# A two-layer graph network: segment sums with h held still, and the destination part of each quad packed on 96 partitions

## The reference

```
m_in  = concat([h_node[src], h_node[dst], h_edge])      # 200000 x 384
m     = silu(m_in @ msg_W1 + msg_b1) @ msg_W2 + msg_b2
agg   = segment_sum(m, dst, 6250)
h_new = silu(concat([h_node, agg]) @ upd_W1 + upd_b1) @ upd_W2 + upd_b2
x1    = layernorm(x + layernorm(h_node + h_new) * gamma + beta)

agg   = segment_sum(x1[src], dst, 6250) / max(deg, 1)
h     = relu(relu(concat([x1, agg]) @ W1 + b1) @ W2 + b2)
out   = layernorm(x1 + h)
```

## Time and profile before

| | us |
|---|---|
| median of 3 runs | 3071.88 |
| lowest, highest | 3070.5, 3090.59 |
| span of the profiled execution | 2569.7 |
| preparation (0 to 82) | 82 |
| edge stage (82 to 2095) | 2013 |
| edge stage's end (2095 to 2107) | 12 |
| node stage and layer 1 (2107 to the end) | 463 |

### The profile page before, as it was taken

The page is one execution under the profiler, slowest core; times in us unless marked ns, Lnnn a source line. Parts: engine busy times, 40 slices in busy tenths (PEclk is TensorE's granted clock), DMA queues, the critical chain, the costliest instruction groups (busy, mean ns, idle before and its releaser), DMA issues. The chain is left out here.

```text
span 2569.7 us, 58924 instructions
## 1 busy us (share of the span) xinstructions
PE 2182.9 (85%) x21030; PEld 1871.4 (73%) x21030; DVE 1577.3 (61%) x4059; ACT 847.9 (33%) x1368; POOL 1664.2 (65%) x1618
## 2 busy tenths in 40 slices
PE   7898888888888988898889888988898878799996
PEld 7786777677777776776777776767677754699994
DVE  4786676667666766676667666766676647600005
ACT  3343333333333433333333333333333326200004
POOL 4777777777777777777777777777777755200002
PEclk9899999899899989998899999999999988899998
DMA  6555545554555555545554555455545543688871
GB/s 236 197 190 190 167 159 185 181 169 154 177 190 173 158 180 181 187 141 180 184 190 139 186 175 190 144 182 176 191 150 176 176 118 96 245 309 302 303 268 51
DMA packets 135225, 471.71 MB, mean 184 GB/s; under 512 B 55730, under 2 KB 77490, under 8 KB 113555
## 3 DMA queue, kind: packets, MB, share of 16 engines
q1 hardware_dynamic: 84586, 368.35, 41.1%
q0 software_dynamic: 50176, 102.86, 14.3%
q10 hardware_dynamic: 426, 0.03, 0.0%
HBM read 369.41 MB, written 101.70 MB: 183 GB/s over the span
## 5 line engine op out<-in xcount | busy, mean ns | idle before, releaser
L519 POOL DMA_INDIRECT gath<-P_d,src_i x1540 | 1543.2, 1002 | 469.4 <-issue 465.5
L650 PE MATMUL ps_pre<-wc,eT 128*128 128x128 f32 x3136 | 702.4, 306 | 13.7 <-DVE counts L567 13.7
L682 PE MATMUL ps_sum<-h,edgeN 128*128 128x129 f32 x3136 | 486.2, 302 | 265.7 <-ACT h L744 265.2
L590 DVE TENSOR_TENSOR pre<-ps_pre,gath 128x512 f32<-128x512 f32 x392 | 265.9, 678 | 588.6 <-issue 548.7
L682 PEld LDWEIGHTS ps_sum<-h,edgeN 128*128 128x128 f32 x3136 | 422.2, 209 | 278.1 <-ACT h L744 277.7
L744 ACT ACTIVATE h<-pre 128x512 f32<-128x512 f32 x392 | 247.9, 632 | 1122.2 <-DVE pre L590 1068.3
L666 PE MATMUL ps_cnt<-edgeK,edgeL 128*128 128x500 bf16 (+1 forms) x3136 | 585.1, 336 | 29.6 <-DVE edgeK L580 29.4
L580 DVE TENSOR_SCALAR edgeK<-iota,key 128x600 bf16<-128x600 f16 (+2 forms) x1568 | 526.4, 396 | 0.0
L652 PE MATMUL ps_pre<-Qw,nodeE 128*128 128x128 bf16 x4704 | 520.4, 220 | 0.0
L650 PEld LDWEIGHTS ps_pre<-wc,eT 128*128 128x128 f32 x3136 | 478.1, 192 | 32.6 <-issue 29.6
L666 PEld LDWEIGHTS ps_cnt<-edgeK,edgeL 128*128 128x128 bf16 x3136 | 320.1, 105 | 199.3 <-DVE edgeK L580 42.8
(11 more groups left out here) (128 smaller groups left out, 1021.4 us busy)
## 6 DMA issues: line engine op xcount, KB each, us to landing
eT<-eT SPq DMA_DIRECT2D x56, 1792.0 KB, 9.2
A_d<-counts SPq DMA_DIRECT2D x56, 1568.0 KB
A_c<-A_d SPq DMA_DIRECT2D x56, 1568.0 KB, 8.1
rel_b<-rel_d SPq DMA_DIRECT2D x56, 896.0 KB
gath<-P_d,src_i POOLq DMA_INDIRECT x1568
Qw<-Q_d SPq DMA_DIRECT2D x56, 96.0 KB
Q_d<-Qst SPq DMA_DIRECT2D x7, 672.0 KB, 7.8
xT_sb<-xT SPq DMA_DIRECT2D x7, 448.0 KB, 8.1
```

Of the source, the lines that this page charges most:

```text
L519: pool.indirect_dma_start(gath[:, q, t * D:(t + 1) * D], None, v["P_d"], bass.IndirectOffsetOnAxis(ap=src_i[k][:, c:c + 1], axis=0)).then_ ...
L590: V.tensor_tensor(pre[x][:], ps_pre[x][:], gath[:, q, :], ALU.add).then_inc(pre_add, 1)
L650: T.matmul(o, eT[k][:, e0:e0 + P], wc[:], start=True, stop=False)
L682: last = T.matmul(ps_sum[k][:, 0:SW], edgeN[x][:, t, :], h[x][:, t, 0:SW], start=(q == 0 and t == 0), stop=(q == GQ - 1 and t == QT - 1))
```

## The change

- **Sums.** `h` is now held still and a one-hot moves: per tile one f32 product of `h` with 40 columns of `edgeN` (f32), so that the sums come out with features on partitions, as `sumT` wants them. `edgeN` covers 40 nodes from `NLO[q]`, not 128. Degrees come from four more products, of a matrix of ones with `edgeB`, the same one-hot in bf16. A product of zeros clears the bank first. ACT's copy of the sums, the transposes and the column of ones are gone. `add_sums` reads the bank itself, at quad 1 of the next group, not at quad 5.
- **One-hot of the block.** `edgeL` is made by four TENSOR_SCALARs of 128 columns.
- **Destination part.** The window is 32 nodes per quad, and its 96 partitions hold (node, part) pairs: partition p holds part p mod 3 of node p // 3. One product of K = 96 takes the place of three. `rel_d` is relative to the quad's first node; `pid` holds p // 3. `nodeE` is made per quad (`expand`, 96 x 512), two quads ahead. `Qw` is loaded by seven DMAs per group, each with its own read of a row number (`qbase`). `rel_b` has two buffers of 96 partitions.
- **Checks.** Each quad has to lie in its 40-node window.

```diff
@@ sizes
+QW = 32
+WN = 40
+NLO = [max(0, 16 * q - 10) for q in range(GQ)]
+KQ = 3 * QW
@@ build_prepare, vector: checks
-            V.tensor_scalar(relR[:], R_i[:, 0:RC], RB_i[:, 0:1], None, ALU.subtract).then_inc(rel_ready, 1)
+            V.tensor_tensor(rows4(relR[:]), rows4(R_i[:, 0:RC]),
+                            RB_i[:].unsqueeze(2).broadcast_to([RP, RQ, QT * P]), ALU.subtract).then_inc(rel_ready, 1)
...
+            for q in range(GQ):
+                V.tensor_scalar(bad[:, 5, q:q + 1], dF[:, q:q + 1], float(NLO[q]), None, ALU.is_lt)
...
+            V.tensor_scalar(qbase[:], orow[:], 3.0, None, ALU.mult)
@@ build_edges, sync
         def load_window(g, k):
 
-            base = sp.value_load(gbase[0:1, bass.ds(g, 1)], min_val=0, max_val=NP_ - 1)
-            sp.dma_start(Qw[k][:], v["Q_d"][bass.ds(base, P), :]).then_inc(q_in[k], 16)
+            for q in range(GQ):
+                base = sp.value_load(qbase[0:1, bass.ds(g * GQ + q, 1)], min_val=0, max_val=3 * NP_ - 3)
+                sp.dma_start(Qw[k][:, q, :], Q3[bass.ds(base, KQ), :]).then_inc(q_in[k], 16)
...
-                    sp.wait_ge(prepared, g + 2)
-                    load_rel(g + 2)
+                    sp.wait_ge(nodes, g * GQ + GQ)
+                    load_rel(g + 2, k)
@@ build_edges, vector
+        def expand(s, q, k, half, first=False):
+
+            x = (k + q) % 2
+            if q == 0:
+                dve.wait_ge(r_in[k], 16 * (half + 1))
+            if not first:
+                dve.wait_ge(pre_mm, s - 1)
+            V.tensor_scalar(nodeE[x][:], rel_b[k][:, q * QT * P:(q + 1) * QT * P], pid[0:KQ, 0:1], None,
+                            ALU.is_equal).then_inc(nodes, 1)
...
-            V.tensor_tensor(edgeN[x][:], io, rel_g[k][:, c].unsqueeze(2).broadcast_to([P, QT, P]), ALU.is_equal)
-            V.tensor_tensor(edgeL[x][:], io, low[k][:, c].unsqueeze(2).broadcast_to([P, QT, P]), ALU.is_equal)
+            io = iota[:, NLO[q]:NLO[q] + WN].unsqueeze(1).broadcast_to([P, QT, WN])
+            rel = rel_g[k][:, c].unsqueeze(2).broadcast_to([P, QT, WN])
+            V.tensor_tensor(edgeN[x][:], io, rel, ALU.is_equal)
+            V.tensor_tensor(edgeB[x][:], io, rel, ALU.is_equal)
+            for j in range(QT):
+                V.tensor_scalar(edgeL[x][:, j, :], iota[:, 0:P], low[k][:, q * QT + j:q * QT + j + 1], None, ALU.is_equal)
...
-            dve.wait_ge(sum_tr, g + 2)
+            dve.wait_ge(sum_mm, (g + 1) * GQ)
@@ build_edges, tensor
                 T.matmul(o, eT[k][:, e0:e0 + P], wc[:], start=True, stop=False)
-                for part in range(3):
-                    last = T.matmul(o, nodeE[k][:, e0:e0 + P], Qw[k][:, part * D:(part + 1) * D],
-                                    start=False, stop=(part == 2))
+                last = T.matmul(o, nodeE[x][:, t * P:(t + 1) * P], Qw[k][:, q, :], start=False, stop=True)
...
             for t in range(QT):
-                last = T.matmul(ps_sum[k][:, 0:SW], edgeN[x][:, t, :], h[x][:, t, 0:SW],
-                                start=(q == 0 and t == 0), stop=(q == GQ - 1 and t == QT - 1))
+                T.matmul(ps_sum[k][:, cols], h[x][:, t, :], edgeN[x][:, t, :], start=False, stop=True, skip_group_check=True)
+            for t in range(QT):
+                last = T.matmul(ps_sum[k][:, P + NLO[q]:P + NLO[q] + WN], onesb[:], edgeB[x][:, t, :], start=False, stop=True,
+                                skip_group_check=True)
```

More of the change, by code:

```diff
@@ L279, in scalar @@
         firsts, lasts = v["dst_first"], v["dst_last"]
[L280 to L283, removed]
+        with nc.allow_non_contiguous_dma(reason="one word for each quad"):
+            act.dma_start(RB_i[:], firsts[0:TILES].rearrange("(r q t) -> r q t", q=RQ, t=QT)[:, :, 0]).then_inc(r_in, 16)
         act.dma_start(F_i[:], bass.AP(firsts.tensor, firsts.offset, [[GT, GROUPS], [1, GT + 1]])).then_inc(t_in, 16)
@@ L418, in build_edges @@
     first_i = [v["first_i0"], sb("first_i1", [P, GT], I32)]
-    nodeE = [sb(f"nodeE{k}", [P, GE], BF16) for k in range(2)]
-    Qw = [sb(f"Qw{k}", [P, 3 * D], BF16) for k in range(2)]
+    rel_b = [v["rel_b0"], sb("rel_b1", [KQ, GE], BF16)]
+    nodeE = [sb(f"nodeE{k}", [KQ, QT * P], BF16) for k in range(2)]
+    Qw = [sb(f"Qw{k}", [KQ, GQ, D], BF16) for k in range(2)]
     rel_g = [sb(f"rel_g{k}", [P, GT]) for k in range(2)]
@@ L425, in build_edges @@
     low = [sb(f"low{k}", [P, GT]) for k in range(2)]
-    edgeN = [sb(f"edgeN{k}", [P, QT, P]) for k in range(2)]
+    edgeN = [sb(f"edgeN{k}", [P, QT, WN]) for k in range(2)]
+    edgeB = [sb(f"edgeB{k}", [P, QT, WN], BF16) for k in range(2)]
     edgeL = [sb(f"edgeL{k}", [P, QT, P], BF16) for k in range(2)]
@@ L606, in group @@
                 add(s, q, k, g, first and q < 2)
+                if q < GQ - 2:
+                    expand(s + 2, q + 2, k, half)
+                elif not last:
+                    expand(s + 2, q + 2 - GQ, nxt[1], nxt[0])
                 if q < GQ - 1:
@@ L611, in group @@
                     hots(s + 1, 0, 1 - k)
-                if not last and q in (2, 3, 4):
-                    if q == 2:
-                        make_keys(*nxt)
-                    else:
-                        (expand_first, expand_rest)[q - 3](*nxt, early=first)
-                if q == 5 and not first:
+                if not last and q == 2:
+                    make_keys(*nxt)
+                if not last and q == 3:
+                    clear(*nxt, early=first)
+                if q == 1 and not first:
                     add_sums(g - 1, 1 - k)
         def fast():
-            for k in range(2):
-                V.memset(h[k][:, :, D:D + 2], 1.0).then_inc(h_ones, 1)
             dve.sem_inc(sum_add, 1)
             make_keys(0, 0, first=True)
-            expand_first(0, 0, early=True)
-            expand_rest(0, 0, early=True)
+            clear(0, 0, early=True)
+            expand(0, 0, 0, 0, True)
+            expand(1, 1, 0, 0, True)
             dve.wait_ge(prepared, 1)
@@ L704, in group @@
                     count(s + 1, 0, k1, g + 1)
-                if q == 1 and not first:
-                    transpose_sums(g - 1, 1 - k)
         def fast():
-            pe.sem_inc(sum_tr, 1)
-            pe.wait_ge(h_ones, 2)
             products(0, 0, 0, 0, True)
```

117 lines of the change are left out of this document (55 added, 62 removed).

## The result

The changed kernel took 3180.09 us (median of 4, 3172.81 to 3189.22) and the kernel before, beside it, 3072.57 (4 runs, 3070.50 to 3090.59): ratio 1.0328, 95% interval 1.0290 to 1.0365. Forecast were 3026 us and a range of 2996 to 3066. The prediction was wrong, in sign too.

What follows compares the result with a forecast made beforehand. The prediction took POOL's back-to-back gathers to bound the edge stage: 49 us less of their waits for VectorE and 3.5 us more at the start make -46 us, so 3026 us from 3071.9, range 2996 to 3066.

Steps and rivals of the forecast that it cites:

- The median of the runs, 3071.9, is 502 us more, which I keep: Whole run: the 502 us between the traced span of 2569.7 us and the median were kept unchanged in the forecast.
- The stage is POOL's row of gathers, back to back: Edge stage: 1540 gathers of 1.002 us, each with 0.305 us before it, make its 2013 us; other engines wait.
- A gather that begins while such an instruction runs waits for that instruction's end, and then goes ahead of the next one: Edge stage, gathers beside VectorE: each waits for one instruction's rest, less about 0.12 us; in all 88 us before.
- The forecast's term: Edge stage: gathers' waits for VectorE instructions fall from 88 to 39 us, 49 us less.
- upper end: Edge stage: gathers' waits after the change are 70 us if nothing falls into step any more, 17 us less.
- If a gather's start fell anywhere at random: Edge stage: an instruction of length L costs (L - 0.126)^2 / (2 x 1.247) us; sums scaled by 0.55.
- The rule of the Trainium skill: Gathers beside VectorE: TENSOR_TENSORs do not stall them, two-port TENSOR_SCALARs do; the sum would be -2 us, not -46.
- The start: Group 0: six more window loads on SP make POOL's first gather of group 1 3.5 us later, once.
- PE's and ACT's savings worth nothing: Edge stage: removed products, transposes and ACT's copy of the sums give 0 us, since the gathers cover them.
- rival 1: Edge stage: new VectorE instructions run without gaps, gathers meet edgeK more, waits fall only 17 us; 3058 us, chance 0.20.
- Rival 3: Edge stage: more idle time lowers PE's clock to 0.65 and PE becomes the bound, +118 us; 3190 us, chance 0.07.

Runs made afterwards that it cites:

- quiet sets: No change to a kernel: sets of runs in which the kernel before took about 2569 us, named after what their traces show.
- halting set: No change to a kernel: a set of runs in which the kernel before took 3072 to 3129 us, named after what its traces show.
- eight products back: Changed kernel with eight more bf16 products per quad on TensorE, onto the same sums with a right side of zeros; 1.0447 of the kernel before.

## Experiments in quiet sets: what the prediction was about

**Instructions added to VectorE's row** (one set, before 2568.92).

```diff
 expand_per_quad             # kernel before; nodeE [P, 512] twice, PE waits for it per quad
+                expand(s + 2, q + 2, k, half)      # behind each add, 128x512
-                        (expand_first, expand_rest)[q - 3](*nxt, early=first)
 vector_034_more             # kernel before
                 add(s, q, k, g, first and q < 2)
+                V.tensor_scalar(spare[3 * k + q % 3][:], iota[:, 0:QT * P], pid[:, 0:1], None, ALU.is_equal)
 expand_bulk                 # changed kernel; nodeE [KQ, GE], two instructions per group
+                        (expand_first, expand_rest)[q - 3](*nxt, early=first)
 no_gathers                  # kernel before; groups 1 to 55 use group 0's rows
-                    pool.indirect_dma_start(
```

> The kernel before with nodeE built per quad, 512 columns right behind each add, where TensorE waits for it, in place of two instructions of 1792 columns per group; three products and one window load stay. The destination part alone cost 144 us, while its eight fewer products gave 39 and seven window loads cost 20, so some 160 us are unexplained. Theory V (a VectorE instruction put into every quad between the add and the one-hots lengthens the chain add, one-hots, counts, add): 0.34 us x 392 = 133 us more, ratio about 1.04 to 1.05. Theory S (only SyncE's loads, the clear and the store cost): within 1% of before. Theory F (each engine starves for instructions now and then, and the number of instructions sets the loss): 5 more VectorE instructions per group, within 1%.

> The kernel before with one VectorE TENSOR_SCALAR of 512 columns more behind each add, into a tile that nobody reads and nobody waits for. Theory V: 0.34 us x 392, ratio 1.03 to 1.045, since the one-hots and so TensorE's counts come later by that. Theory F: one instruction more on VectorE per quad, ratio 1.00 to 1.015. If VectorE has slack, as its 56% of busy time says: 1.00.

> The changed kernel with nodeE built as before in two instructions of 1792 columns per group (on 96 partitions), and the clear of the counts back at the fifth quad. Theory V: 100 us or more come back, ratio to before 0.99 to 1.00. Theory S: the later clear takes the 93 us of waiting for the A_d store away: 1.00 to 1.015. Theory F: no change against the changed kernel, 1.033.

> The kernel before without the gathers of groups 1 to 55 (the adds use group 0's rows, so the result is wrong). In the unchanged kernel run again TensorE's stutters (single matmuls 0.7 us apart with 'issue' gaps, 463 us in the edge stage, in some 130 clusters) end with the last gather. Theory G (POOL's gathers starve the other engines of instructions): no stutter is left, and the edge stage falls from 2485 to 392 x 4.1 = 1610 us, a time near 2200 us. Theory F without the gathers' part: the stutters stay, one cluster in about 110 TensorE records, and the time stays near 3070 us, since the rows are there 35 us before the add anyway.

Measured: 1.0244 (1.0226 to 1.0262), 1.0186 (1.0168 to 1.0205), 1.0241 (1.0223 to 1.0259), 0.832 (0.8303 to 0.8337). This set had no halts, so theories G and F were not put to the test. Theory V's figures, 1.03 to 1.05 for the first two, did not come either: 63 and 46 us, not 133. What the set shows is the quiet kernel: without gathers the time is 431 us less, so the gathers do set the end there.

**The change itself, in a quiet set** (before 2568.23).

> The changed kernel unchanged. If the kernel before takes about 2570 us beside it: theory H (gathers wait through whole rows of back-to-back VectorE instructions, so mean gather 1.04 instead of 1.002) gives 2570 + 60 = 2630 us, as expand_bulk did; the forecast's own theory (a gather waits only for the instruction in which it begins) gives 2524 us; theory K (clock) 2690. If the kernel before takes over 3000 us: 1.033 of it again.

> The destination part alone, unchanged. Without stutters, theory H: expand_per_quad's 1.024 plus what SyncE's window loads add, 1.02 to 1.04. With stutters: 1.048 again.

> The kernel before with the sums part (h stationary, 40 columns) and the block one-hot by four TENSOR_SCALARs, without the destination part. Without stutters, theory H: the four short TENSOR_SCALARs and edgeK stand back to back for 1.9 us per quad, but nodeE is built as before: 1.00 to 1.015; the forecast's theory 0.98. With stutters: the parts gave 1.019 and 1.009 alone, so 1.028 if they add up, less if stutters cost by time and not by part.

> The kernel before without the gathers of groups 1 to 55, unchanged. Without stutters: 0.832 again. With stutters in the kernel before: if they need the gathers, no stutter is left and the time is 2137 us as before, ratio 0.69; if they do not, some 130 stretches stay and the time is 2400 to 3000 us.

Measured: the changed kernel 2840.46 us, 1.1054 (1.1027 to 1.1081); destination part alone 2978.4, 1.1607 (1.1557 to 1.1657); sums and block 0.9974 (0.9957 to 0.9991); no_gathers 0.8313 (0.8295 to 0.833). The change costs 272 us here and 108 in the halting set: it is dearer where my model of the kernel holds. None of the expected figures for it (2630, 2524, 2690 us) came near, nor theory H's 1.02 to 1.04 for the destination part. The kernel before takes the same time in this set and in the one above (2568.23, 2568.92), so expand_bulk may be put beside the changed kernel: it has the same windows, products and sums, with the expansion in two instructions per group and the clear a quad later, and 210 of the 272 us are gone. The page's rows of the gathers, in the order sums_and_block, expand_per_quad, changed kernel, destination part:

```profile
L532 POOL DMA_INDIRECT gath<-P_d,src_i x1540 | 1529.8, 993 | 469.5 <-issue 461.0
```

```profile
L520 POOL DMA_INDIRECT gath<-P_d,src_i x1540 | 1611.4, 1046 | 469.3 <-issue 466.3
```

```profile
L542 POOL DMA_INDIRECT gath<-P_d,src_i x1540 | 1815.6, 1179 | 470.9 <-issue 463.3
```

```profile
L543 POOL DMA_INDIRECT gath<-P_d,src_i x1540 | 1940.8, 1260 | 471.8 <-issue 460.5
```

POOL's idle time stays 470 us, the fixed 0.30 us. The mean gather alone moves the span, by 1540 times its difference from the earlier trace rows (the spans are of one profiled run each; the medians of sums_and_block and vector_034_more lie 5.7 us below and 46 us above the kernel before):

| kernel | mean gather, ns | 1540 x difference, us | span less 2569.7, us |
|---|---|---|---|
| sums_and_block | 993 | -14 | -13.8 |
| vector_034_more | 1030 | +43 | +37.7 |
| expand_bulk | 1040 | +59 | +61.1 |
| expand_per_quad | 1046 | +68 | +64.9 |
| changed kernel | 1179 | +273 | +271.2 |
| destination part | 1260 | +397 | +399.6 |

The median stays at 944 to 947 ns in all of them; single gathers get long. Gathers over 1.5 us: 9 in the kernel before, 21 in expand_per_quad, 279 in the changed kernel, 373 in the destination part. What these take beyond 0.945 us each makes 314 us in the changed kernel and 480 in the destination part. The timelines show two gathers that begin at the same place of the same row, 0.27 us into edgeN. First expand_per_quad, where it takes 1.23 us:

```profile
1002.04 0.69 DVE L590 TENSOR_TENSOR pre<-ps_pre,gath 128x512 f32<-128x512 f32 x1 [8.10 <-issue]
1002.64 0.39 DVE L560 TENSOR_SCALAR nodeE<-rel_b,pid 128x512 bf16<-128x512 bf16 x1
...
1002.95 0.67 DVE L577 TENSOR_TENSOR edgeN<-iota,rel_g 128x512 f32<-128x512 f16 x1
1003.22 1.23 POOL L520 DMA_INDIRECT gath<-P_d,src_i  x1 [0.30 <-issue]
...
1003.55 0.68 DVE L578 TENSOR_TENSOR edgeL<-iota,low 128x512 bf16<-128x512 f16 x1
1004.15 1.36 DVE L580 TENSOR_SCALAR edgeK<-iota,key 128x1000 bf16<-128x1000 f16 x4
```

Then the destination part, 1.91 us:

```profile
1005.56 0.69 DVE L613 TENSOR_TENSOR pre<-ps_pre,gath 128x512 f32<-128x512 f32 x1 [2.70 <-issue]
1006.17 0.41 DVE L589 TENSOR_SCALAR nodeE<-rel_b,pid 96x512 bf16<-96x512 bf16 x1
...
1006.50 0.67 DVE L600 TENSOR_TENSOR edgeN<-iota,rel_g 128x512 f32<-128x512 f16 x1
1006.77 1.91 POOL L543 DMA_INDIRECT gath<-P_d,src_i  x1 [0.30 <-issue]
...
1007.10 0.68 DVE L601 TENSOR_TENSOR edgeL<-iota,low 128x512 bf16<-128x512 f16 x1
1007.70 1.39 DVE L603 TENSOR_SCALAR edgeK<-iota,key 128x1000 bf16<-128x1000 f16 x4
```

In the first the gather was free at edgeN's end (1.23 - 0.945 = 0.28 us late). In the second it was 0.97 us late, held through edgeN and edgeL to about edgeL's end. They are no exceptions: 126 gathers of expand_per_quad begin 0.25 to 0.3 us into edgeN and are 0.27 to 0.30 us late, 162 of the destination part do and are 0.94 to 1.83 us late. Nor is being held through a row the changed kernel's own: 8 gathers of the kernel before that begin in edgeN are some 1.12 us late, and 14 of expand_per_quad that begin in nodeE some 2.4 us, with all instructions on 128 partitions.

**Partitions** (one set, halting, before 3080.63). The two rows differ in nodeE's partitions, 128 and 96, besides the window loads and the products.

```diff
 expand_96                   # expand_per_quad; nodes 96 to 127 are left out of nodeE
-            V.tensor_scalar(nodeE[x][:], rel_b[k][:, ...], pid[:, 0:1], None,
+            V.tensor_scalar(nodeE[x][0:96, :], rel_b[k][0:96, ...], pid[0:96, 0:1], None,
 after_128                   # changed kernel; rel_b and nodeE on 128 partitions, PE reads 96
-            V.tensor_scalar(nodeE[x][:], rel_b[k][:, ...], pid[0:KQ, 0:1], None,
+            V.tensor_scalar(nodeE[x][:], rel_b[k][:, ...], pid[:, 0:1], None,
```

> expand_per_quad with nodeE's instruction on 96 of the 128 partitions (the other 32 stay zero, so some destination terms are missing); three products, one window load. Theory N (an instruction on 96 partitions in VectorE's row keeps POOL from getting in between the instructions behind it): without stutters some 300 gathers of over 1.5 us and 1.12 to 1.16 of before; with stutters 1.03 to 1.05 and over 150 such gathers. Theory W (the window loads, or TensorE's fewer products, do it): 1.024 again and 21 such gathers.

> The changed kernel with rel_b and nodeE on all 128 partitions (the products read 96 of them). Theory N: without stutters the long gathers go (279 to under 60) and the time falls from 1.105 of before to 1.00 to 1.03; with stutters from 1.033 to 1.00 to 1.03. Theory W: 1.105 (or 1.033) again.

Measured: 1.0305 (1.0267 to 1.0344) and 1.0331 (1.0297 to 1.0365). Gathers over 1.5 us: expand_96 172, against 21 in expand_per_quad (a quiet set; it has no trace of a halting one) and 23 in the unchanged kernel of a halting set; after_128 110, against the changed kernel's 209. The number of partitions moves them in both directions, as theory N has it, but a half stays with 128, so it is not the only cause. In time after_128 gave nothing here (1.0331 against 1.0328), which fits a last gather that ends 37 us before its add; what it gives in a quiet set was not measured.

## Why the prediction was wrong

**"The median of the runs, 3071.9, is 502 us more, which I keep": failed.** The time is the span and about 2 us. The 502 us lay inside the edge stage, nearly all, with PE's halts. I took a difference that no row explained for a constant; it was the sign that trace and median came from different conditions.

**"The stage is POOL's row of gathers, back to back": right for the trace, wrong for the median.** In quiet sets the table above has every kernel's span within 6 us of what the gathers' mean gives. In halting sets PE's halts set the pace, and POOL waits.

**"A gather that begins while such an instruction runs waits for that instruction's end, and then goes ahead of the next one": this step failed for the change in quiet sets.** In the kernel before it mostly holds (a gather 0.25 to 0.3 us into edgeN takes 0.28 us more, and only 26 of 1540 lose over 0.5 us). In the changed kernel 281 gathers do. The forecast's term was 88 to 39 us, and its upper end 70; measured are 88 to 360 (1540 x (1.179 - 0.945)), 314 of them in the 279 long gathers. Why a gather is let in at one instruction's end and held through several at another stays open; expand_bulk shows that 210 us of the cost hang on the short expansion in every quad (and on the clear's place, which went back with it). The trace ahead had the warning in the earlier trace rows, a longest gather of 3097 ns, which that rule can't give with no instruction over 0.72 us. I read the median and the mean and not the maximum.

**"If a gather's start fell anywhere at random": failed too.** vector_034_more adds one instruction of 0.34 us per quad, by the formula 385 x 0.0185 x 0.55 = 4 us, and cost 38 in span. By the timelines the cause is the phase: the add starts when the last gather's rows have landed, and the next gather but one starts 1.2 us later; 0.34 us put in between moves edgeN under it. In the kernel before 13 gathers begin 0.25 to 0.3 us into edgeN, in vector_034_more 111, in expand_per_quad 126.

**The rule of the Trainium skill** ("SBUF — State Buffer", "Who interferes with whom") that I weighed, by which only TENSOR_SCALARs would hinder: the gathers held by edgeN and edgeL, both TENSOR_TENSORs, speak against it again (77 of the kernel before's 88 us are lost by gathers that begin in one of these two, 12 by those that begin in the edgeK TENSOR_SCALARs). By it the exchange gives nothing, and that was nearer to the result than my -49 us, though for another reason.

**The start: right.** PE's first product at 80.60 and the first gather of group 1 at 84.92 in the quiet set, 2.4 us later than in the earlier trace rows; forecast 3.5. **PE's and ACT's savings worth nothing: right** in quiet sets (PE waits 451 us for ACT's h there, 262 before), and in halting ones nearly so. **The sums and block parts** took 5.7 us off the median in a quiet set (13.8 between single spans), the sign forecast and little of the size: by the forecast's formula they take the waits from 0.414 to 0.206 us per quad, 44 us. Here rival 1's mechanism is at work: gathers that begin in edgeN and edgeL lose 77 us before and 20 in sums_and_block (edgeB with them), but those that begin in edgeK lose 52 us instead of 12. Rival 1 still had 17 us of gain from it for the whole change, and no loss.

**Rival 3, PE's clock, 3190 us**, comes within 10 us of the median, and should not be credited for it in full: I had it in a kernel without halts, where at 0.82 PE still waits for its rows. In halting sets its mechanism is real (clock 0.84 to 0.74, 214 us of work taken away and 20 of busy time), but the stage's added 95 us are 108 of PE's named waits (42 to 150) and 8 of issue gaps, less 18 of busy time and 3 of small gaps. I had the clock make PE the bound, and there PE was busy for no longer than before; that the number agrees is in good part luck.

Open are: what makes a set halting (one chip gave both kinds, 3129 and 2568 us); whether halts need the gathers (they end with the last one, but so does the loop, and both runs without gathers fell into quiet sets); what besides the partitions lets VectorE's row hold a gather over several instructions; and how the parts' costs in halting sets, 230 us alone and 101 together, combine.

## What to carry to other kernels

Put the profiled execution's span beside the median before anything else: where they differ by more than a few us, the trace isn't of the runs that will be compared, and a sum worked out on it needs a second one for the other condition. Where a queue of gathers shares time with VectorE, forecast its waits by their phase behind the event that starts the row, and look at the longest gather, not the mean; a short instruction put at the head of the row can cost more than its own length. Taking work off an engine may give back little where its clock falls with its activity and others hold it up as soon as it is faster: here 3136 matmuls, 207 us of work at full clock, were worth 38 us.

## What the runs showed of the hardware

- Halts: PE's matmuls 0.7 or 1.4 us apart in 126 stretches of a 2485 us stage, 463 us of issue gaps, VectorE, ACT and SP late with them, POOL not; on one chip in one set and not in another; one stretch for each 97 to 140 of PE's records, or 16 to 25 us, in 11 kernels.
- A gather's surplus over 0.945 us beside VectorE: mostly the rest of one instruction, but over 0.55 us in 279 gathers of the changed kernel and up to 2.7 us in the destination part, through up to eight back-to-back instructions. With nodeE on 96 partitions there were 172 such gathers (over 1.5 us) in a kernel that had 21 with 128, in a quiet set; back from 96 to 128 they went from 209 to 110 in the changed kernel, both in halting sets.
- PE's granted clock in the edge stage went with its work at full clock: 0.74 (changed), 0.79 (eight products back, or eight fewer in the kernel before), 0.84 (before), all in halting sets.
